# Six transposes dealt out in twos between the three products of a projection

## The reference, cut to what matters

```python
def local_attn(x, Wqkv, Wout):
    qkv = x @ Wqkv.T
    q, k, v = jnp.split(qkv, 3, axis=-1)
    ...                                   # windows of 64; keys and values of the window and its two neighbours
    sim = jnp.einsum('bhnid,bhnjd->bhnij', q, ke) * SCALE
    ...
    attn = jax.nn.softmax(sim, axis=-1)
    o = jnp.einsum('bhnij,bhnjd->bhnid', attn, ve)
    return o @ Wout.T
...
light = local_attn(_ln(x, ln_w, ln_b), Wqkv, Wout_l)
```

## Time and profile before

| what | value |
|---|---|
| median of 3 runs | 1855.6 us (1853.57 to 1856.98) |
| the profiled execution's own time | 1859.21 us |
| its span, first to last instruction | 1857.4 us |
| mean granted clock of TensorE, as a share of full speed | 0.976 |
| busy, share of the span: PE / PEld / DVE / ACT / POOL | 91% / 70% / 78% / 77% / 41% |
| first transposes of the first and of the last half tile, stage f1l | 503.99 and 998.81 us |
| first transposes of the first and of the last half tile, stage f2l | 1241.52 and 1731.14 us |

### The profile page before, as it was taken

The page is one execution under the profiler, slowest core; times in us unless marked ns, Lnnn a source line. Parts: engine busy times, 40 slices in busy tenths (PEclk is TensorE's granted clock), DMA queues, the critical chain, the costliest instruction groups (busy, mean ns, idle before and its releaser), DMA issues. The chain is left out here.

```text
span 1857.4 us, 67964 instructions
## 1 busy us (share of the span) xinstructions
PE 1684.3 (91%) x27513; PEld 1292.5 (70%) x27513; DVE 1448.5 (78%) x3468; ACT 1436.0 (77%) x4092; POOL 753.7 (41%) x842
## 2 busy tenths in 40 slices
PE   3888899886999999999997996989999999999797
PEld 1444444443688888888886774658888888888686
DVE  8999999998577778777887766747777777789574
ACT  4989999996588888888774666668888888877464
POOL 2010000000145444545445866425454545455685
PEclk7999999998999999999999998999999999999999
DMA  6655555551001010101012000000000010101211
GB/s 196 147 142 149 151 132 136 143 141 24 13 14 26 14 26 14 26 14 26 14 24 49 2 2 1 1 12 20 20 20 20 16 23 17 23 14 25 48 46 47
DMA packets 80040, 91.94 MB, mean 49 GB/s; under 512 B 11697, under 2 KB 67985, under 8 KB 79729
## 3 DMA queue, kind: packets, MB, share of 16 engines
q1 hardware_dynamic: 78432, 87.15, 19.2%
q10 hardware_dynamic: 1296, 0.44, 0.1%
HBM read 39.68 MB, written 31.10 MB: 38 GB/s over the span
## 5 line engine op out<-in xcount | busy, mean ns | idle before, releaser
L1497 POOL TENSOR_TENSOR f1l_pn<-f1l_p,f1l_rs 128x512 f32<-128x512 f32 (+1 forms) x256 | 207.9, 834 | 259.6 <-DVE f1l_rs L1185 258.6
L1497 POOL TENSOR_TENSOR f2l_pn<-f2l_p,f2l_rs 128x512 f32<-128x512 f32 (+1 forms) x256 | 207.9, 834 | 250.7 <-DVE f2l_rs L1185 250.7
L1065 ACT ACTIVATE f2l_p<-f2l_sm,f2l_nb 128x192 f32<-128x192 f32 x512 | 214.4, 443 | 44.5 <-DVE f2l_nb L1178 44.5
L1065 ACT ACTIVATE f1l_p<-f1l_sm,f1l_nb 128x192 f32<-128x192 f32 x512 | 214.5, 443 | 42.4 <-DVE f1l_nb L1178 42.4
L412 PE MATMUL r_acc<-r_pr,r_vp 128*32 128x128 f32 (+2 forms) x3584 | 193.3, 332 | 6.6 <-DVE r_pr L625 5.5
L522 ACT ACTIVATE r_pr<-r_far 128x1536 f32<-128x1536 f32 x128 | 194.7, 1521 | 2.9 <-PE r_far L396 2.6
L617 DVE SCALAR_TENSOR_TENSOR r_pr<-r_pr,k_lo,r_cap 128x512 f32<-128x512 f32 x256 | 179.8, 743 | 9.0 <-ACT r_pr L522 8.8
L625 DVE TENSOR_SCALAR r_pr<-r_pr,k_hi,k_lo 128x768 f32<-128x768 f32 x256 | 163.1, 678 | 0.0
L522 ACT ACTIVATE r_pr<-r_near 128x1024 f32<-128x1024 f32 x128 | 138.9, 1085 | 1.4 <-PE r_near L383 1.3
L1502 POOL MEMSET k_rtz<- 128x608 f32 x1 | 0.6, 605 | 334.3 <-POOLq L683 334.3
L1178 DVE TENSOR_REDUCE f2l_nb<-f2l_sm 128x4 f32<-128x768 f32 x128 | 116.0, 947 | 7.5 <-PE f2l_sm L885 7.5
(11 more groups left out here) (503 smaller groups left out, 5173.4 us busy)
## 6 DMA issues: line engine op xcount, KB each, us to landing
rbf_rows<-r_part SPq DMA_DIRECT2D x112, 128.0 KB, 2.2
r_qs<-rbf_rows SPq DMA_DIRECT2D x60, 192.0 KB
r_ks<-rbf_rows SPq DMA_DIRECT2D x60, 192.0 KB
f1l_vs<-f1l_vv SPq DMA_DIRECT2D x64, 128.0 KB, 2.4
f2l_vs<-f2l_vv SPq DMA_DIRECT2D x64, 128.0 KB, 2.4
rbf_rows<-r_part SPq DMA_DIRECT2D x16, 384.0 KB, 3.0
rbf_rows<-r_part SPq DMA_DIRECT2D x16, 256.0 KB, 3.1
out<-k_x SPq DMA_DIRECT2D x8, 512.0 KB, 3.2
```

The costliest lines, as they stand in the source:

```text
L1065: ins = nc.scalar.activation(p[:, u % 2, k, :], sm[:, u % 2, k // 2, k % 2 * PW:(k % 2 + 1) * PW], ACT.Exp, bias=nb[:, u % 2, k:k + 1], ac ...
L1497: ins = nc.gpsimd.tensor_tensor(pn[:, u % 2, at:at + HU * w].rearrange("p (k c) -> p k c", k=HU), p[:, u % 2, :, cols], r.broadcast_to([P, ...
```

## The change

A projection of `use` gets a third argument, a function that is called after each of its three products. `turn` is split in `turn_ready` (its waits for `pn` and `tp`) and `turn_third`, whose parts 0 and 1 are two transposes into `tp` each and whose part 2 holds the waits for `s_oe` and `s_ps` and the two transposes into `xa`. `use_and_turn` calls `turn_ready` first and then a projection with two transposes after each of its products. Both half tiles of a step are dealt out in that way, into `use(3i+1)` and `use(3i+2)`. All four chunks of `output` stand together between them, in every step. `values(2t)` now stands ahead of `use(3i+3)`. ACT takes `leave_late(2t)` ahead of `leave(3i+3)`, and DVE takes `residual(t-1)` at the same place in every step. The number of instructions on each engine stays what it was.

```diff
@@ PE: use @@
                     nc.tensor.matmul(at, w_l[:, w], xh[:, par, :], start=True, stop=False)
+                    between(0)
                     nc.tensor.matmul(at, w_h[:, w], xh[:, par, :], start=False, stop=False)
+                    between(1)
...
-                    mm = nc.tensor.matmul(at, w_h[:, w], xl[:, par, :], start=False, stop=True)
+                    nc.tensor.matmul(at, w_h[:, w], xl[:, par, :], start=False, stop=True).then_inc(s_pp, 1)
+                    between(2)
@@ PE: turn, in parts @@
+            def turn_third(n, part):
+                u = n % UNITS
+                if part < 2:
+                    for k in (2 * part, 2 * part + 1):
+                        nc.tensor.transpose(tp[:, k * P:(k + 1) * P], pn[:, u % 2, k * P:(k + 1) * P], K["ident"][:])
+                    return
                 wait(pe, s_oe, n - n % 2)
                 wait(pe, s_ps, n)
...
+            def use_and_turn(b, k, n):
+                turn_ready(n)
+                use(b, k, lambda part: turn_third(n, part))
@@ PE: step @@
-                ahead = i == TURN_AT and b + 2 < B
                 if more:
-                    use(b + 1, 3 * i + 1)
-                turn(2 * t)
-                output(t - 1, (0,) if ahead else (0, 1))
+                    use_and_turn(b + 1, 3 * i + 1, 2 * t)
+                else:
+                    turn(2 * t)
+                output(t - 1, (0, 1, 2, 3))
                 if more:
-                    use(b + 1, 3 * i + 2)
-                if not ahead:
-                    output(t - 1, (2, 3))
-                turn(2 * t + 1)
-                if ahead:
-                    output(t - 1, (1,))
+                    use_and_turn(b + 1, 3 * i + 2, 2 * t + 1)
+                else:
+                    turn(2 * t + 1)
+                values(2 * t)
                 if more:
                     use(b + 1, 3 * i + 3)
-                if ahead:
-                    output(t - 1, (2, 3))
+                if i == TURN_AT and b + 2 < B:
                     turn_x(b + 2)
-                values(2 * t)
                 if t + 2 < T:
                     scores(2 * t + 4)
                     scores(2 * t + 5)
@@ ACT: step @@
+                leave_late(2 * t)
                 if more:
                     leave(b + 1, 3 * i + 3)
                 if i == TURN_AT and b + 2 < B:
                     leave_x(b + 2)
-                leave_late(2 * t)
@@ DVE: step @@
-                late = t % NT == TURN_AT and t // NT + 2 < B
-                if t and not late:
+                if t:
                     residual(t - 1)
...
-                if late:
-                    residual(t - 1)
```

More of the change, by code:

```diff
@@ L825, in _, with use @@
         def _(pe):
-            def use(b, k):
+            def use(b, k, third=None):
                 at, par = bank(b, k), b % 2
+                between = third or (lambda part: None)
                 if b == 0 and (k <= 2 * HP or not C):
@@ L845, in use @@
                     nc.tensor.matmul(at, xl[:, par, rows], w_h[:, w], start=True, stop=False)
+                    between(0)
                     nc.tensor.matmul(at, xh[:, par, rows], w_l[:, w], start=False, stop=False)
-                    mm = nc.tensor.matmul(at, xh[:, par, rows], w_h[:, w], start=False, stop=True)
-                mm.then_inc(s_pp, 1)
+                    between(1)
+                    nc.tensor.matmul(at, xh[:, par, rows], w_h[:, w], start=False, stop=True).then_inc(s_pp, 1)
+                    between(2)
             def turn_x(b):
@@ L888, in scores, with turn_ready @@
                 mm.then_inc(s_sm, 1)
-            def turn(n):
+            def turn_ready(n):
                 b, par, u = place(n)
@@ L898, in turn @@
                 wait(pe, s_pt, n)
-                for k in range(HU):
-                    nc.tensor.transpose(tp[:, k * P:(k + 1) * P], pn[:, u % 2, k * P:(k + 1) * P], K["ident"][:])
+            def turn_third(n, part):
[4 more added lines that the diff above has]
+                    return
                 wait(pe, s_oe, n - n % 2)
@@ L906, in turn @@
                 mm.then_inc(s_t, 1)
+            def turn(n):
+                turn_ready(n)
+                for part in range(3):
+                    turn_third(n, part)
+            def use_and_turn(b, k, n):
+                turn_ready(n)
+                use(b, k, lambda part: turn_third(n, part))
             def values(n):
```

## The result

The changed kernel takes 1975.2 us in the median against 1856.3 for the kernel before, 119 us more. The measured ratio is 1.0625, with a 95% interval of 1.0603 to 1.0647, a little less than the quotient of these medians; by it the loss is 116 us, and so it is between the two profiled executions (1975.1 and 1859.2 us). Forecast had been +125 and 1981, so the time is inside the range.

The account below looks back on a forecast made before the run. PE sets the pace while projections run. Step terms gave 115 us, 129 with the constants, less 4: +125 on the profiled 1859.2 us, 1984, put at 1981 against the median; range 1940 to 2008.

Parts of the forecast that it names:

- Part 1: Weight loads of transposes dealt out between a projection's products: one load hidden in either order, gain 0.
- Part 2: values(2t), now ahead of use(3i+3), loses the projection that covered DVE's copy: +0.98 us a step.
- Part 3: Between the two half tiles, the second projection waits for the copy from tp with only output as cover: +0.10 us.
- Part 4: Start of the step, where the last two transposes wait for leave_values on DVE: -0.05 us, between 0 and -0.14.
- Steps with i = 2: Steps whose old order had turn_x and a use between last transpose and values: +0.75 us each.
- Part 5: First light stage: DVE's constants, covered before, now land in PE's wait for the copy from tp: 14 us, between 0 and 18.
- The sum: Two light stages, 15 batches: 115 us, 129 with the constants, less 4 for waits already there: +125 us.
- Two loads: Rival: two loads hide behind each product, 0.3 us a step, 36 in all, 1945 us; chance 0.07.
- free rides: Rival: a product hides both its transposes whole, -0.28 us a step, -34 in all, 1822 us; chance 0.04.
- the swallowed waits: Rival: both DVE copies come in time, 1855 to 1864 us; chance of ending within 0.2%: 0.03.
- the falling clock: Rival: PE idles some 0.9 us a step and its clock falls, some 50 us more, 2030 us; chance 0.04.
- PE's share: Sign: PE's busy share in the light stages falls from 98% to below 90%, at a clock of 1.00.

## Why the prediction was right

**Part 1, loads, 0.** Held in the sum: a dealt-out pair and its product take 0.46, and the steps with i = 0 and 1 did not change when one half tile was dealt out alone. The split was another than the one that the prediction named as a sign: the next product starts 0.03 behind the second transpose, not 0.23 (1381.87 + 0.11 to 1382.01), and the transposes 0.32 behind the product (to 1382.33). The rule of the Trainium skill on pulling loads ahead (TensorE: Matmul & The Clock Gate, Part 2, step 1) holds here for one load behind the matmul at work; no run shows a second.

**Part 2, +0.98 a step.** Held: last transpose to values 0.87 (0.88 forecast from step 62), the last small matmul of values to scores 1.05 (1.05), and 0.97 a step where this line was moved alone. The last steps of a stage, which have no projections, had shown the bare wait in the trace of before; that row carried the forecast.

**Part 3, +0.10.** Too large: last transpose to last transpose is 2.44 (1382.94 to 1385.38) instead of 2.42, so +0.02. The copy starts 0.34 after the transposes, as said, but the projection follows it by 0.77 (1383.28 to 1384.05), not by 0.83, and from there to the sixth transpose it takes 1.33, not 1.35. The prediction had expected an idle there that ends with that copy; the profile marks none. What the copy costs shows against the bunched order of the change: 0.19 a step.

**Part 4, -0.05.** 1.41 from the step's start to its sixth transpose, -0.08.

**Steps with i = 2, +0.75.** From first transpose to first transpose such a step of the second stage took 8.33 in the median before and takes 9.05: +0.72.

**Part 5, 14 us.** The first stage lost 13.5 us more than the second. Moving the constants behind both copies wins 11 of them back. Moving them between the copies wins nothing, which I had not foreseen; that they grow there would explain it.

**The sum.** Per step with i = 1: forecast 7.69 + 1.03 = 8.72, measured 8.64. The forecast let this step stand for those with i = 0 and 3 also. In the medians of the second stage the three came out at +0.99 (i = 0), +0.93 (i = 1) and +1.08 (i = 3), 1.00 on average; that the errors of the single steps nearly cancel is luck. The stage as a whole grew by 53 us, some 3 less than its medians add up to: the kernel before had some longer steps of its own, so the 4 us taken off for waits already there were rather too few.

**The rivals and the signs.** Two loads and free rides fall by the 0.46, the swallowed waits by 34.1 us of them in one stage, the falling clock by 1.00 in both windows. In the last steps of the second stage the clock did stand lower (0.92 from 1820 to 1842 us), and there the last four steps took 25.4 us instead of 23.9. PE's share was to fall from 98% to below 90%; it did so in the first stage (89%), not in the second (93%).

## What to carry to other kernels

Before an instruction stream is made denser, ask what the bunch was covering: here six transposes in a row covered an eviction by ACT, and the projection behind them covered a copy by DVE. Dealing the transposes out bares the first (values back behind the projection, all dealt out), and moving `values` ahead bares the second. A wait taken off one place on a saturated engine is won only if no other place is short of the same cover, so look for a stretch of the old trace in which the cover is already missing and read the price there. Where a half of a result is needed first, produce and count that half first: it won back 70 of the 116 us without moving anything else.

## What I had not expected of the hardware

The constants are small, yet they grew when they were moved: those on DVE between 640 and 860 us last 21 us added up in the changed kernel, 47 between the copies and 42 behind both. Here is one instruction, a scaling of 128x512 numbers in SBUF, in three kernels, with POOL's normalising beside it where there was any.

In the changed kernel, DVE, with POOL idle from 724.67 to 729.50:

```profile
727.57 0.47 DVE L1337 TENSOR_SCALAR k_c_dec<-k_c_dec,k_c_mag 128x512 f32<-128x512 f32 x1
```

With the constants between the copies, DVE (up to the copy from `xa`) and POOL:

```profile
725.61 1.30 DVE L1337 TENSOR_SCALAR k_c_dec<-k_c_dec,k_c_mag 128x512 f32<-128x512 f32 x1
...
727.19 0.41 DVE L1209 COPY f1l_pt<-f1l_xa 128x256 f32<-128x256 f32 x1
```

```profile
725.58 1.79 POOL L1510 TENSOR_TENSOR f1l_pn<-f1l_p,f1l_rs 128x512 f32<-128x512 f32 x2 [4.35 <-DVE f1l_rs L1201]
```

With the constants behind both copies:

```profile
726.25 0.46 DVE L1337 TENSOR_SCALAR k_c_dec<-k_c_dec,k_c_mag 128x512 f32<-128x512 f32 x1
```

```profile
726.41 1.76 POOL L1510 TENSOR_TENSOR f1l_pn<-f1l_p,f1l_rs 128x512 f32<-128x512 f32 x2 [1.12 <-DVE f1l_rs L1201]
```

Where POOL starts 0.03 us ahead, DVE's 0.47 becomes 1.30; where DVE starts 0.16 ahead, DVE keeps its 0.46 and POOL's pair takes 1.76 where a pair without a constant beside it takes 1.61 (that at 723.68, for one). The Trainium skill (SBUF — State Buffer, Who interferes with whom) says that DVE in its two-port mode and POOL share a pair of ports which the first to issue holds for its whole instruction; these rows agree, though none shows in which mode DVE was. The constants are placed close behind `reciprocals`, and `reciprocals` is what starts POOL's normalising, so in either new place they run into it. This is read from the rows and was not tried by itself; it would explain why the place between the copies won nothing, though DVE had 1.15 us free there, and why the last place won 10 or 11 us and not 13.
